# P products interleaved with the update of the node features, and a count product 128 rows deep

## The reference

```python
h = x
for _ in range(2):
    edge_input = concatenate([h[src], h[dst], edge_attr], axis=-1)     # 128 + 128 + 32
    m_ij = relu(edge_input @ We1 + be1) @ We2 + be2
    h = h + segment_sum(m_ij, dst, num_segments=N)
h = h + bias
x = layernorm(x + h)
# then: gcn_conv with degree-normalised edge weights, relu, residual, layernorm
```

## Time and profile before

| | us |
|---|---|
| median of three runs | 2439.45 |
| the profiled execution, whole | 2436.7 |
| its span, first to last instruction | 2434.5 |
| TensorE products busy | 2195.3 (90%) |
| GpSimd busy | 1700.0 (70%) |
| VectorE busy | 1396.8 (57%) |
| ScalarE busy | 895.7 (37%) |

### The profile page before, as it was taken

One profiled execution on the slowest core, in us unless ns is written; L12 is line 12 of the kernel. 1 busy time (PEld: TensorE's weight loads), 2 busy tenths in 40 slices (PEclk: granted clock), 3 DMA queues, 4 the chain that ended last, 5 costly groups with the idle time before them and its releaser, 6 DMA issues.

```text
span 2434.5 us, 49886 instructions
## 1 busy us (share of the span) xinstructions
PE 2195.3 (90%) x14876; PEld 1723.8 (71%) x15066; DVE 1396.8 (57%) x3830; ACT 895.7 (37%) x1461; POOL 1700.0 (70%) x1772
## 2 busy tenths in 40 slices
PE   2899999999999998899999999999998679999996
PEld 2677676666666666676666666666666579999996
DVE  2765555655555542465555555555553467777875
ACT  2443334444443432243434444433434332322322
POOL 3677777777777775277777777777777377677763
PEclk8899999999999995699999999999998689999998
DMA  5333333333333332333333333333333211111111
GB/s 143 88 105 100 102 102 101 102 102 102 102 101 101 102 97 86 100 90 101 102 101 102 102 98 100 102 100 100 102 101 101 64 48 51 49 49 49 48 47 50
DMA packets 156158, 218.67 MB, mean 90 GB/s; under 512 B 73955, under 2 KB 107609, under 8 KB 155950
## 3 DMA queue, kind: packets, MB, share of 16 engines
q0 software_dynamic: 56272, 115.27, 18.4%
q1 hardware_dynamic: 92638, 98.41, 14.1%
q10 hardware_dynamic: 7168, 4.09, 0.7%
HBM read 207.48 MB, written 10.12 MB: 89 GB/s over the span
## 4 chain that ended last, share of the span: by engine, by line
POOL 45%; issue 29%; PE 18%; DMA 3%; DVE 3%; ACT 1%; POOLq 1%; SPq 0%; DVEq 0%; ACTq 0%
POOL gat L524 44%; PE ps L709 6%; PE ps L718 6%; PE ps L595 3%; DMA gat<-dst_row 1%; PE ps L792 1%; DMA gat<-p_dram,idx 1%; DMA gat<-z_dram,idx 1%; PE ps L788 1%; DMA cbase_dram<-cint 0%; PE ps L658 0%; PE ps L634 0%; DVE node_a L1206 0%; PE ps L618 0%; PE ps L584 0%
## 5 line engine op out<-in xcount | busy, mean ns | idle before, releaser
L524 POOL DMA_INDIRECT gat<-p_dram,idx x1422 | 1364.0, 959 | 471.4 <-issue 430.7
L658 PE MATMUL ps<-node_a,x 128*128 128x512 bf16 x2210 | 679.9, 382 | 11.0 <-issue 1.1
L1225 DVE TENSOR_TENSOR msg<-ps,gat 128x512 f32<-128x512 f32 (+1 forms) x404 | 252.8, 627 | 680.6 <-DMA gat<-p_dram,idx 592.3
L595 PE MATMUL ps<-hot,msg 128*128 128x64 f32 x3232 | 449.3, 287 | 99.7 <-ACT msg L910 86.6
L1206 DVE TENSOR_SCALAR node_a<-ps,row_id 128x512 bf16<-128x512 f16 x1200 | 486.5, 475 | 47.2 <-PE ps L641 35.3
L595 PEld LDWEIGHTS ps<-hot,msg 128*128 128x128 f32 x3232 | 408.9, 200 | 129.6 <-ACT msg L910 108.9
L658 PE MATMUL ps<-node_a,adj 128*128 128x512 bf16 x1200 | 458.6, 382 | 0.0
L584 PEld LDWEIGHTS ps<-rhs,lhs 96*128 96x128 f32 x3232 | 408.7, 199 | 53.8 <-ACT lhs L891 23.4
L584 PE MATMUL ps<-rhs,lhs 96*128 96x128 f32 x3232 | 412.6, 283 | 24.4 <-ACT lhs L891 16.5
L524 POOL DMA_INDIRECT gat<-z_dram,idx x328 | 321.9, 982 | 160.4 <-issue 100.7
L658 PEld LDWEIGHTS ps<-node_a,x 128*128 128x128 bf16 x2400 | 237.0, 102 | 243.7 <-issue 9.4
(11 more groups left out here) (154 smaller groups left out, 1787.8 us busy)
## 6 DMA issues: line engine op xcount, KB each, us to landing
dbc<-dst_row SPq DMA_DIRECT2D x202, 256.0 KB
lhs<-eaT SPq DMA_DIRECT2D x202, 128.0 KB
gat<-p_dram,idx POOLq DMA_INDIRECT x1422
rhs<-q_dram SPq DMA_DIRECT2D x202, 32.0 KB
gat<-z_dram,idx POOLq DMA_INDIRECT x328
idx<-src_g SPq DMA_DIRECT2D x243, 4.0 KB
p_dram<-node_a ACTq DMA_DIRECT2D x12, 256.0 KB
q_dram<-node_b SPq DMA_DIRECT2D x12, 256.0 KB, 3.5
```

The lines of the kernel that those rows point to most:

```text
L524: return pool.indirect_dma_start(out=out_, out_offset=None, in_=table, in_offset=bass.IndirectOffsetOnAxis(ap=index, axis=0))
L595: last = nc.tensor.matmul(ps_agg(s), (msg if p < 2 else gat)[s][:, c, :], hot[s][:, c, (0 if p < 2 else 1), :], start=(c == 0), stop=(c == ...
L658: mm = nc.tensor.matmul(ps_own, p_part[k][:, t, :], shot[j % 2][:, t - t0, :, :].rearrange("p j e -> p (j e)"), start=(t == 0 and k == 0), ...
L1225: V.tensor_tensor(msg[s][:, c0:c1, :], ps_pre(s, h)[:, 0:(c1 - c0) * P].rearrange("p (c f) -> p c f", f=P), gat[s][:, c0:c1, :], ALU.add). ...
```

## The change

- **Order on TensorE.** The P products of pass 1 no longer stand in the table stage. In the update loop, from its third round on, each round makes count product b, update product b, and then the P pair of block b − 2; two more rounds finish the P pairs. The Q pairs follow as before.
- **PSUM banks.** Count products use banks 0 and 1, update products of pass 0 banks 2 and 3, P pairs of pass 1 banks 4 to 7, Q pairs of pass 1 banks 0 to 3. Count and update products now wait for the addition two blocks earlier. The wait for the last count addition stands behind the loop.
- **Depth.** `be2_row` and `cw` get 128 rows (they are cleared on all rows at the start), and the count product uses all 128; the rows past the fourth are zero. The degree products and the additions into `cw` keep their four rows.

```diff
-        be2_row = sb("be2_row", [4, P])
+        be2_row = sb("be2_row", [P, P])
-        cw = sb("cw", [4, NPAD])
+        cw = sb("cw", [P, NPAD])
...
+            def p_products(p, j):
+                if p:
+                    pe.wait_ge(m_added, j + 1)
+                if j >= 4:
+                    pe.wait_ge(p_copied, 13 * p + j - 3)
+                for t in (2 * j, 2 * j + 1):
...
+                    mm = nc.tensor.matmul(ps[:, P_BANK[p] + j % 4, (t % 2) * P:(t % 2 + 1) * P],
+                                          hT[:, t * P:(t + 1) * P], wpq[:, 0, :], start=True, stop=True)
+                mm.then_inc(p_mm, 1)
...
                 def counted(b):
-                    if b >= 4:
-                        pe.wait_ge(cb_added, b - 3)
-                    nc.tensor.matmul(ps[:, b % 4, 0:BLK], be2_row[:, :], cw[:, b * BLK:(b + 1) * BLK],
+                    if b >= 2:
+                        pe.wait_ge(cb_added, b - 1)
+                    nc.tensor.matmul(ps[:, b % 2, 0:BLK], be2_row[:, :], cw[:, b * BLK:(b + 1) * BLK],
                                      start=True, stop=True).then_inc(cb_mm, 1)
...
                     pe.wait_ge(agg_clear, 1)
-                    for b in range(NBLK):
-                        counted(b)
-                        if b >= 4:
-                            pe.wait_ge(m_added, b - 3)
-                        updated(b)
+                    for b in range(NBLK + 2):
+                        if b < NBLK:
+                            counted(b)
+                            if b >= 2:
+                                pe.wait_ge(m_added, b - 1)
+                            updated(b)
+                        if b >= 2:
+                            p_products(1, b - 2)
+                    pe.wait_ge(cb_added, NBLK)
```

More of the change, by code:

```diff
@@ L23 @@
 OWN_AT = CH - 1
+P_BANK = (0, 4)
+Q_BANK = (4, 0)
 PARTS4 = [(0, 6), (6, 6), (12, 6), (18, 7)]
@@ L602, in scatter_products, with q_products @@
                 return sum_products(p, s, 0, CH)
+            def p_products(p, j):
[4 more added lines that the diff above has]
+                for t in (2 * j, 2 * j + 1):
+                    if p == 0 and t % PIECES[0][1] == 0:
+                        pe.wait_ge(x_in[t // PIECES[0][1]], 16)
+                    mm = nc.tensor.matmul(ps[:, P_BANK[p] + j % 4, (t % 2) * P:(t % 2 + 1) * P],
+                                          hT[:, t * P:(t + 1) * P], wpq[:, 0, :], start=True, stop=True)
+                mm.then_inc(p_mm, 1)
+            def q_products(p, j):
+                if j >= 4:
+                    pe.wait_ge(q_copied, 13 * p + j - 3)
+                for t in (2 * j, 2 * j + 1):
+                    mm = nc.tensor.matmul(ps[:, Q_BANK[p] + j % 4, (t % 2) * P:(t % 2 + 1) * P],
+                                          hT[:, t * P:(t + 1) * P], wpq[:, 1, :], start=True, stop=True)
+                mm.then_inc(q_mm, 1)
             for p in range(3):
                 if p < 2:
-                    for a, copied, done in ((0, p_copied, p_mm), (1, q_copied, q_mm)):
+                    if p == 0:
                         for j in range(TILES // 2):
[L609 to L620, removed]
+                            p_products(0, j)
+                    for j in range(TILES // 2):
+                        q_products(p, j)
                     pe.wait_ge(p_copied, 13 * (p + 1))
@@ L633, in _ @@
                     for t in range(TILES):
-                        mm = nc.tensor.matmul(ps[:, 7, t:t + 1], cw[:, t * P:(t + 1) * P], parts[:, 0:1],
+                        mm = nc.tensor.matmul(ps[:, 7, t:t + 1], cw[0:4, t * P:(t + 1) * P], parts[:, 0:1],
                                               start=True, stop=True)
@@ L785, in counted @@
                 def counted(b):
-                    if b >= 4:
-                        pe.wait_ge(cb_added, b - 3)
-                    nc.tensor.matmul(ps[:, b % 4, 0:BLK], be2_row[:, :], cw[:, b * BLK:(b + 1) * BLK],
+                    if b >= 2:
+                        pe.wait_ge(cb_added, b - 1)
+                    nc.tensor.matmul(ps[:, b % 2, 0:BLK], be2_row[:, :], cw[:, b * BLK:(b + 1) * BLK],
                                      start=True, stop=True).then_inc(cb_mm, 1)
                 def updated(b):
-                    nc.tensor.matmul(ps[:, 4 + b % 4, 0:BLK], we2[:, :], aggT[:, b * BLK:(b + 1) * BLK],
+                    nc.tensor.matmul(ps[:, 2 + b % 2 if p == 0 else 4 + b % 4, 0:BLK], we2[:, :], aggT[:, b * BLK:(b + 1) * BLK],
                                      start=True, stop=True).then_inc(m_mm, 1)
@@ L862, in _ @@
                         nc.scalar.copy(node_a[:, 2 * j:2 * j + 2, :],
-                                       ps[:, j % 4, 0:2 * P].rearrange("p (t f) -> p t f", t=2)
+                                       ps[:, P_BANK[p] + j % 4, 0:2 * P].rearrange("p (t f) -> p t f", t=2)
                                        ).then_inc(p_copied, 1)
@@ L1119, in _ @@
                         V.tensor_tensor(node_b[:, 2 * j:2 * j + 2, :],
-                                        ps[:, 4 + j % 4, 0:2 * P].rearrange("p (t f) -> p t f", t=2),
+                                        ps[:, Q_BANK[p] + j % 4, 0:2 * P].rearrange("p (t f) -> p t f", t=2),
                                         be1_bc[:, :].unsqueeze(1).to_broadcast([P, 2, P]), ALU.add
@@ L1165, in add_window @@
                         if p == 0:
-                            c = cw[:, bass.ds(b, W)]
+                            c = cw[0:4, bass.ds(b, W)]
                             V.tensor_tensor(c, c, ps_cw(s), ALU.add)
@@ L1353, in _ @@
                             if p == 0:
-                                V.tensor_tensor(cw[:, bass.ds(w * W, W)], cw[:, bass.ds(w * W, W)],
+                                V.tensor_tensor(cw[0:4, bass.ds(w * W, W)], cw[0:4, bass.ds(w * W, W)],
                                                 ps_cw(0), ALU.add)
@@ L1368, in _ @@
                         dve.wait_ge(cb_mm, b + 1)
-                        V.tensor_tensor(xTs[:, cols], ps[:, b % 4, 0:BLK], xTs[:, cols], ALU.add).then_inc(cb_added, 1)
+                        V.tensor_tensor(xTs[:, cols], ps[:, b % 2, 0:BLK], xTs[:, cols], ALU.add).then_inc(cb_added, 1)
                         dve.wait_ge(m_mm, b + 1)
                         dve.wait_ge(cb_added, b + 1)
-                        V.tensor_tensor(hT[:, cols], ps[:, 4 + b % 4, 0:BLK], xTs[:, cols], ALU.add
+                        V.tensor_tensor(hT[:, cols], ps[:, 2 + b % 2, 0:BLK], xTs[:, cols], ALU.add
                                         ).then_inc(m_added, 1)
```

## The result

The changed kernel takes 2421.81 us (median of four runs, 2420.82 to 2422.84) against 2440.13 for the kernel before; the ratio is 0.993 with a 95% interval of 0.9918 to 0.9943. That is 18.3 us, where 18.0 were forecast; the interval stands for 13.9 to 20.0.

What follows compares the result with a forecast made beforehand. TensorE alone was taken to bound the 43.7 us stretch before the degree products; equal depth and a faster clock would bring these from 1006.33 to 988.3, 18.0 us off the 2439.45 median: 2421.4 us, range 2416.5 to 2429.5.

Steps and rivals of the forecast that it cites:

- What bounds: Update block and table stage before pass 1: TensorE alone sets the 43.7 us stretch; order alone brings nothing.
- The 0.30 us at a change of depth: Old update block: alternating 4-row and 128-row products costs 0.30 us per change, 26 times, 7.8 us; equal depths remove it.
- rival A: Rewritten stretch: clock rises but weight loads stay exposed, rounds 1.60 to 1.90 us, gain 12.3 us, 2427.1 us; chance 0.07.
- The clock: Update block: without 4-row products the clock rises 4.2 us after the first count product, bounds 2 to 7 us.
- The sum: Start of the degree products: they come at 988.3 instead of 1006.33, a gain of 18.0 us.
- The clearing of `aggT`: Before GpSimd's first gather of pass 1: 2.87 us, ending 1.5 us after P, hidden by the later last store.
- What follows: After the degree products: the 18.0 us gain passes whole through pass 1, give or take 3 us.
- Rival D: Pass 1: the clock or the gathers take back about half the gain, 2430 us; chance 0.09.
- B: Rewritten stretch: clock stays at 0.50 until the Q products, rounds 2.56 us, gain 2.4 us, 2437 us; chance 0.06.
- Rival C: Rewritten stretch: clock low and loads exposed, rounds 3.15 us, degree products 5.3 us late, 2444.7 us; chance 0.04.

Runs made afterwards that it cites:

- Depth_only: The kernel before, in its old order and banks, with only the count product made 128 rows deep; 2421.63 us, ratio 0.9931 to the kernel before.
- order_only: The changed kernel with its new order and banks, but the count product on 4 rows as before; 2439.43 us, ratio 1.0012 to the kernel before.

## Why the prediction was right, and where it was not

- **What bounds.** The stretch hangs on TensorE alone: shown. Depth_only and order_only give the cross-check: without its depth the order loses 4.7 us in the stretch; without the order the depth keeps all but 0.8 at the same rise of the clock.
- **The 0.30 us at a change of depth.** Right in size: 0.85 us from product to product in the changed kernel. Wrong in the reason, "equal depths": 96 rows cost nothing beside 128, 64 cost the full 0.30. The Trainium skill ("TensorEngine Tiling (Array Packing)", Key Properties) says that changing the tiling mode drains the engine, and (When to Use Tiling, Row Tiling) gives a contract dimension of 64 or less as the case for row tiles. The runs agree with a drain between those two classes: 0.30 us at the lower clock for 4 and 64 rows, none for 96. That a product of 64 rows is such a mode of its own, no run shows. The rule on weight loads behind rival A is not borne out: the load at 962.85 is hidden between two products on the same 128 rows, and the load that is not hidden, at 963.75 in the kernel before, stands between products on different rows.
- **The clock.** Right that it rises, and that the shallow products held it. The step that it came after 4.2 us was mis-sized: 5.0 in the first profile, 3.2 to 5.6 over the seven profiles of this order with 96 or 128 rows, each microsecond worth 0.50 us. The bounds of 2 to 7 held. A slip in the reading bears on nothing: the page's two low slices are 913 to 1035 us, one slice later than the prediction has them, and the windows that it goes on with are right.
- **The sum.** Rounds of 1.31 us on the mean (1.30 forecast), Q from 981.87 (981.8), degree products at 988.45 (988.3). The block began 0.35 us earlier than before, so that the stretch gained 17.5 us instead of 18.0. The clearing of `aggT` ended at 983.64, 2.5 us ahead of the first gather: hidden, as forecast.
- **What follows.** The gain went through: the first message addition and GpSimd's wait there moved by 17.9 us (1036.96 to 1019.09), the medians by 18.3. Rival D did not come, and neither did A (rounds of 1.6 to 1.9) or B (clock down to the Q products). That the median came within 0.3 us of the 18.0 is luck in part: the interval is 6 us wide, and the stretch alone gained 17.5.
- **Rival C**, run as order_only, had the right stretch (rounds of 3.15 us, 48.5 against 49.0). Its end, 5.3 us slower, is not excluded by an interval from 0.7 less to 6.6 more, but its step that all goes through was wrong: 2 us came back in the degree products, which ran in the main at the other clock level.

## What to carry to other kernels

A product of 4 or 64 rows among products of 128 cost twice here: 0.30 us at each change at the lower clock, and a granted clock that stayed at its lower level through some 40 us in which TensorE's row shows no pause. Padding such a product with zero rows cost no time (0.85 us a product at either depth), and it is worth trying before any reordering. Where one engine works a stretch through without a gap, look at the clock row before looking for overlap: the new order alone made this stretch 4.7 us longer, and on top of the depth it brought 0.8.

## What the runs showed of the hardware that was not expected

The line lies between 64 and 96 rows, both for the pause (0.30 us and none) and for the clock (0.50 for 38 us, and up after 5.6). A row of 64-row products, 0.87 us apart, leaves the clock at 0.50 for 11.7 us. Under products of one column it falls at 128 rows too, after 2.1 us, though weight loads keep the engine busy.

Depth is not all that decides. Late in pass 0 of the changed kernel TensorE makes only products of 96 and 128 rows from 928.57 to 936.04, and is busy nearly throughout: 16 instructions with 64 columns each in 3.7 us, then 16 with 128 columns in 3.7. The clock stays at 0.50:

```profile
928.50:936.00 7.50, 7.39 (x35) 6.98 (x32) 2.00 (x6) 2.78 (x4) 5.98 (x6) 0.50 0.44 112
```

What a change of depth costs at the upper level no run shows, since the clock never rose in a stream that had one.
